# One fused decoder layer on one core: the shared step table is replaced by a table of its own for each engine

## The chip, the core and the metric

The kernel runs on one NeuronCore of a Trainium2 chip. The metric is the device time of one execution in microseconds; smaller is better. All data are fp32. Five engines take part: TensorE (PE, with its weight loads as PEld), VectorE (DVE), ScalarE (ACT), GpSimd (POOL) and SyncE (SP), which issues most DMAs.

## The reference, cut to what matters

```
x: (16, 128, 256)   ctx_1024: (16, 128, 256)          # 16 sequences of 128 tokens, 256 channels
x = x + attn(layernorm(x))        # latent attention: keys = values = x@latent_w (72 wide), 16 heads, causal softmax
x = x + birwkv(r=layernorm(x), k=ctx, v=ctx, w, u)    # two scans along time, sigmoid(r) * wkv
x = x + moe(layernorm(x))         # 8 experts, top 2 by sparsemixer, F=512, silu(gate)*up, down
```

## The kernel before, in words

The batch of 16 sequences is worked in 4 groups g of 4 sequences. Attention is cut into 64 **units** (sequence, quarter of the heads). One unit n runs through five engines: `S.n` scores on PE (mask and 8 matmuls), row maximum on DVE (L1197), four exponentials on ACT (`exps`, L983); `N.n` reciprocal of the sums on DVE (L1201) and the product with the exponentials on POOL (L1593); `T.n` transposes on PE (L739) and copy to `PT` on ACT (L988); `Y.n` mix with the values on PE (L748), copy to `ZT` on DVE (L1212) and, on SP, four DMAs that pack it into `zP` (L574). `O.b.i` is a quarter of the output projection of sequence b. `q.k.i` are five parts of the queries of a pair of sequences k: matmuls into one PSUM bank (L668), a biased copy on ACT (L976), a DMA by head into `qT` on SP (L561). As there is one bank, each part waits for the copy of the one before. `kt.g` and `va.g`/`vb.g` make keys and values.

The rest is threaded between the units. `bn`, `agg`, `rs`, `nmb`, `xn`, `tx` are a layernorm: statistics and shift on DVE, the power on POOL (`rs`, L1588), normalisation on ACT (L950), transposes on PE, copies. `w1` to `w8`, `wa`, `wb` are the bidirectional recurrence of a group and a half of the channels: exponential and scaling on ACT, four scans on DVE (`w2` to `w5`, L1236 and L1238), four sums on POOL (`w6`, `w7`), reciprocals on DVE (`w8`), product on POOL (`wa`), transposes and copy `wb`. `nr`, `sig`, `x2` apply the gate (`sig` is L1026 on ACT). `lg`, `r1` to `r3`, `ra`, `rw` route the tokens; `r4.g...` writes a group's two lists to HBM by eight indirect DMAs from POOL (L1636). After three groups `p1`, `p2`, `p3` plan the expert tiles; POOL then issues `gtk` (token lists, L1668), `gw` (weights of the first tile, L1660) and `lxg` (gathers, L1650). The expert stage with 23 tiles follows (`tg`, `up`, `si`, `hd`, `sh`, `dn`, `ao`, and `sw`, which splits weights: L1048 on ACT, L1132 on DVE), from about 392 us of the span.

The order is written out by hand in one table `STEPS` (L70 to L182), which `schedule()` turns into `ORDER` with a rule for the last tiles. Each of the five engine programs walks `ORDER` from first to last and issues its own part of each step, so all five have the same relative order. An engine is in order: a step that waits for a semaphore holds all its later steps. The count that a semaphore must reach is taken from a step's place in `ORDER` (`nth`).

In `ORDER` the beginning is: statistics, `tx.1.0`, constants, `kt.0`, then `q.0.0` to `q.0.4`, `va.0`, `S.0`, `S.1`, the normalisation of group 1, `S.2`, `T.0`, `q.1.0`, and so on. On POOL the end of the attention stage is: `N.55`, `rs.3.2`, `N.56`, `N.57`, `N.58`, the last two lists of group 1 (`r4.1.0.4.1.2`), `N.59`, `N.60`, six scatters of group 2, `N.61`, its last two, `rs.2.3.0.2`, `N.62`, `N.63`, `gtk.0`, `gtk.1`, `gw.0.0`. On ACT it is `T.60`, `sig.3.0.0`, `T.61`, `T.62`, `sw.0.0`, `T.63`.

## Time and profile before

| what | value |
|---|---|
| median of 3 runs | 604.07 us (602.4 to 605.44) |
| profiled execution | 600.46 us, of it span 598.8 us |
| granted TensorE clock, mean | 0.942 |
| instructions | 10336 |
| HBM read, written | 49.28 MB, 9.49 MB |

The profiled execution is 3.6 us below the median of the three runs. Busy shares stand for each engine; a busy PE is not PE at its peak, since ends of matmuls are modelled, and the weight loads (PEld) are the better measure of how densely the PE queue was fed.

### The profile page before, as it was taken

The numbers are of one execution on the slowest core, as the hardware profiler recorded it, in microseconds if no ns is written. First come the engines' busy times: TensorE is split into PE (matmuls) and PEld (weight loads), VectorE is DVE, ScalarE is ACT, GpSimd is POOL, SyncE is SP. The second block draws the span as 40 slices with busy tenths as digits, with TensorE's granted clock in tenths as the row PEclk, the third lists the DMA queues.
The fourth block names the chain that finished last, engine by engine and source line by source line (L and its number), as shares of the span: only waits on it lengthen the run. The fifth ranks groups of instructions, "written<-read, shape, count | busy, mean of one in ns | idle before, by whom it ended". The sixth has DMA issues, their size and how long they took to land.

```text
span 598.8 us, 10336 instructions
## 1 busy us (share of the span) xinstructions
PE 520.2 (87%) x3448; PEld 453.2 (76%) x3448; DVE 362.9 (61%) x740; ACT 329.9 (55%) x945; POOL 314.7 (53%) x277
## 2 busy tenths in 40 slices
...
GB/s 206 188 43 86 69 93 82 76 72 70 55 119 97 52 67 72 89 82 78 61 42 101 101 176 228 89 124 68 309 167 251 202 241 235 246 236 362 180 19 0
DMA packets 53219, 76.82 MB, mean 128 GB/s; under 512 B 10173, under 2 KB 41662, under 8 KB 52838
## 3 DMA queue, kind: packets, MB, share of 16 engines
...
q8 instruction: 27, 0.44, 0.3%
...
q10 hardware_dynamic: 804, 0.15, 0.1%
HBM read 49.28 MB, written 9.49 MB: 98 GB/s over the span
## 4 chain that ended last, share of the span: by engine, by line
PE 58%; DVE 9%; issue 9%; POOL 9%; DMA 7%; ACT 5%; SPq 2%; POOLq 0%; DVEq 0%; ACTq 0%
PE P L668 18%; PE PO L776 7%; PE P L731 6%; PE P L748 6%; PE PO L668 5%; PE P L739 3%; PE P L852 3%; POOL EB L1593 2%; DMA cxa<-xd,TK 2%; POOL cxa L1650 2%; ACT EB L983 2%; PE PO L861 2%; PE P L727 2%; PE P L686 1%; PE P L792 1%
## 5 line engine op out<-in xcount | busy, mean ns | idle before, releaser
L983 ACT ACTIVATE EB<-P,small 128x128 f32<-128x128 f32 x256 | 90.4, 369 | 74.7 <-DVE small L1197 64.6
L1593 POOL TENSOR_TENSOR EB<-EB,small 128x512 f32<-128x512 f32 x64 | 78.8, 1241 | 86.1 <-DVE small L1201 86.0
L668 PE MATMUL P<-GT,WF 128*128 128x256 f32 x768 | 101.9, 291 | 6.0 <-DVE GT L1132 2.6
L668 PEld LDWEIGHTS P<-GT,WF 128*128 128x128 f32 x768 | 97.4, 198 | 7.2 <-DVE GT L1132 3.1
L1677 POOL DMA_INDIRECT out<-Y,TK x39 | 65.8, 1687 | 65.2 <-DMA out<-Y,TK 29.2
L731 PEld LDWEIGHTS P<-KT,qT 72*128 72x128 f32 x512 | 69.8, 198 | 11.5 <-DMA qT<-qP 6.4
L748 PE MATMUL P<-PT,V 128*72 128x512 f32 x128 | 67.0, 605 | 9.7 <-ACT PT L988 8.2
L731 PE MATMUL P<-KT,qT 72*128 72x128 f32 x512 | 70.3, 282 | 5.1 <-DMA qT<-qP 5.1
L776 PE MATMUL PO<-Ow,zP 128*128 128x256 f32 x270 | 67.5, 390 | 2.7 <-DMA zP<-ZT 2.7
L1212 DVE COPY ZT<-P 72x512 f32<-72x512 f32 x64 | 43.3, 676 | 40.4 <-PE P L748 39.4
L776 PEld LDWEIGHTS PO<-Ow,zP 128*128 128x128 f32 x270 | 50.5, 195 | 15.9 <-issue 10.3
L1197 DVE TENSOR_REDUCE small<-P 128x4 f32<-128x512 f32 x64 | 43.3, 677 | 26.3 <-PE P L731 26.1
L1650 POOL DMA_INDIRECT cxa<-xd,TK x39 | 42.9, 1100 | 30.1 <-DMA TK<-xs 20.0
L668 PE MATMUL PO<-WF,HR 128*128 128x256 f32 x384 | 51.9, 294 | 4.5 <-issue 4.5
L988 ACT ACTIVATE PT<-P 128x512 f32<-128x512 f32 x64 | 38.8, 607 | 27.8 <-PE P L739 27.8
L668 PEld LDWEIGHTS PO<-WF,HR 128*128 128x128 f32 x384 | 49.9, 202 | 4.9 <-issue 4.9
L983 ACT ACTIVATION_READ_ACCUMULATOR EB<-P,small 128x1 f32 x256 | 52.9, 207 | 0.0
L1636 POOL DMA_INDIRECT xs<-TKS,SL x32 | 33.7, 1052 | 35.9 <-DVE TKS L1332 25.6
L739 PEld LDWEIGHTS P<-ident,EB 128*128 128x128 f32 x256 | 31.4, 144 | 22.1 <-issue 10.7
L739 PE MATMUL P<-ident,EB 128*128 128x128 f32 x256 | 39.9, 279 | 4.6 <-POOL EB L1593 4.5
L1077 ACT ACTIVATE Y<-PO,TK 128x256 f32<-128x256 f32 x39 | 16.7, 470 | 38.9 <-DMA out<-Y,TK 15.0
L976 ACT ACTIVATE qP<-P,small 128x256 f32<-128x256 f32 x72 | 30.9, 483 | 12.4 <-PE P L668 12.3
...
## 6 DMA issues: line engine op xcount, KB each, us to landing
WR<-wf SPq DMA_DIRECT2D x27, 512.0 KB, 4.9
arena<-wf SPq DMA_DIRECT2D x24, 512.0 KB, 4.9
...
WS<-wf SPq DMA_DIRECT2D x12, 512.0 KB, 7.8
...
X<-x SPq DMA_DIRECT2D x4, 512.0 KB, 5.9
cxa<-ctxin SPq DMA_DIRECT2D x4, 512.0 KB, 5.2
```

What stands on the lines that cost most here:

```text
L668: r = e.matmul(o, lt(a), rt_(b), start=start and n == 0, stop=stop and n == 2, skip_group_check=skip)
L731: p = e.matmul(S[:, 128 * j:128 * j + 128], qT[k % 2][:, 4 * hq + j, c:c + 128], KT[g % 2][:, r:r + 128], start=False, stop=True, skip_gro ...
L739: p = e.transpose(PTB[:, 128 * j:128 * j + 128], EB[n % 3][:, j, :], ident[:, :])
L748: e.matmul(YB[0:L, :], V[g % 2][:, b % GB, :], PT[n % 2][:, :], start=True, stop=True).then_inc(s_Y, 1)
L776: p = e.matmul(o, zP[b // NB % 2][:, m, 128 * (b % NB):128 * (b % NB) + 128], Ow[:, m, :], start=m == 0, stop=m == NQ - 1)
L983: e.activation(EB[i][:, j, :], S[:, 128 * j:128 * j + 128], ACT.Exp, bias=NM[i][:, j:j + 1], accum_out=SM[i][:, j:j + 1]).then_inc(s_exp, 1)
L988: e.activation(PT[n % 2][:, :], PTB[:, :], ACT.Copy).then_inc(s_pt, 1)
L1197: e.tensor_reduce(NM[n % 3], SB[n % 2][:, :].rearrange("p (h s) -> p h s", h=4), AX.X, ALU.max, negate=True).then_inc(s_max, 1)
L1212: e.tensor_copy(ZT[buf][:, :, c:c + 128], YB[0:L, :].rearrange("p (h t) -> p h t", h=4)).then_inc(s_z, 1)
L1593: e.tensor_tensor(EB[i][:, :, :], EB[i][:, :, :], SM[i].unsqueeze(2).broadcast_to([128, 4, 128]), ALU.mult).then_inc(s_prob, 1)
L1650: e.indirect_dma_start(XG[i][:, a_, :], None, xd[0:(TN * 3 // 4, TN + 1)[phase(j)], :], bass.IndirectOffsetOnAxis(ap=TK[:, j, a_, 0:1].bit ...
L1677: e.indirect_dma_start(outr, bass.IndirectOffsetOnAxis(ap=TK[:, j, a_, 0:1].bitcast(i32), axis=0), Y[j % 2][:, a_, :], None, bounds_check= ...
```

## The change

Five tables are added, `SYNC_STEPS`, `TENSOR_STEPS`, `VECTOR_STEPS`, `SCALAR_STEPS` and `GPSIMD_STEPS`, and a function `steps_of` that parses one. Each engine program walks its own table. `ORDER` and the semaphore counts stay. The steps are the same on every engine (181, 427, 511 of 518, 416 and 185 of them); the seven that are missing on DVE (`tg.16` to `tg.22`) issue nothing there. Against the old order 31, 145, 183, 109 and 47 of them are in another place. From `T.57` on PE, `S.62` on ACT, `Y.60` on DVE, `lxg.1` on POOL and `lw.3.1` on SP the tables are as before. One wait changes, in `add_x1`.

```diff
+SYNC_STEPS = """
+    ctx.0 q.0.0 q.0.1 q.0.2 q.0.3 q.0.4 q.1.0 q.1.1 ctx.1 q.1.2 q.1.3 q.1.4 Y.1 Y.3 Y.5 q.2.0 q.2.1 Y.7 q.2.2 q.2.3 q.2.4 Y.9 Y.11 q.3.0 ctx.2 Y.13
...
+    Y.51 Y.52 Y.53 Y.54 Y.55 out.0.0.4 out.1.0.4 out.2.0.4 xd.2.0.4 Y.56 owh Y.57 Y.58 Y.59 ltk.3 lw.2.0 lw.1.0 lw.1.1 lw.1.2 ltk.4 out.3.0.2 xd.3.0.2
+TENSOR_STEPS = """
+    tx.1.0.0.4.0 tx.1.0.0.4.1 q.0.0 q.0.1 kt.0 q.0.2 q.0.3 q.0.4 q.1.0 va.0 tx.1.1.0.4.0 S.0 S.1 S.2 S.3 S.4 T.0 q.1.1 T.1 Y.0 q.1.2 T.2 Y.1 q.1.3
+    tx.1.1.0.4.1 Y.2 S.5 T.3 q.1.4 S.6 Y.3 S.7 T.4 T.5 q.2.0 kt.1 Y.4 T.6 q.2.1 S.8 S.9 wb.0.0 Y.5 S.10 q.2.2 T.7 Y.6 T.8 S.11 S.12 q.2.3 Y.7 T.9 va.1
...
+VECTOR_STEPS = """
+    bn.1.0.0.0 bn.1.0.0.2 agg.1.0.0.4 nmb.1.0.0.4 split tx.1.0.0.4.0 tx.1.0.0.4.1 consts bn.1.1.0.0 bn.1.1.0.2 agg.1.1.0.4 nmb.1.1.0.4 w1.0.0 w2.0.0
+    w3.0.0 w4.0.0 w5.0.0 vb.0 S.0 S.1 N.0 tx.1.1.0.4.0 N.1 S.2 w1.0.1 N.2 S.3 S.4 w2.0.1 w3.0.1 w4.0.1 Y.0 w5.0.1 w8.0.0.0 w8.0.0.1 Y.1 N.3 w8.0.0.2
+    w8.0.0.3 Y.2 S.5 tx.1.1.0.4.1 N.4 N.5 S.6 N.6 S.7 bn.1.2.0.0 bn.1.2.0.2 Y.3 agg.1.2.0.4 bn.1.3.0.0 bn.1.3.0.2 N.7 Y.4 S.8 S.9 Y.5 w1.1.0 S.10 N.8
...
+SCALAR_STEPS = """
+    xn.1.0.0.0 xn.1.0.0.2 tx.1.0.0.4.0 consts tx.1.0.0.4.1 q.0.0 q.0.1 w1.0.0 w2.0.0 q.0.2 q.0.3 w4.0.0 q.0.4 kt.0 xn.1.1.0.0 xn.1.1.0.2 q.1.0
+    tx.1.1.0.4.0 w1.0.1 S.0 S.1 S.2 S.3 T.0 q.1.1 T.1 q.1.2 T.2 q.1.3 tx.1.1.0.4.1 S.4 T.3 S.5 S.6 q.1.4 T.4 w2.0.1 w4.0.1 T.5 q.2.0 kt.1 S.7 w1.1.0
...
+GPSIMD_STEPS = """
...
+    w7.2.1 N.27 N.28 N.29 x2.0.0.2.0 rs.3.0.0.4 N.30 N.31 N.32 N.33 wa.2.1 N.34 w6.3.0 N.35 N.36
+    N.37 N.38 N.39 w7.3.0 xb.6 N.40 N.41 wa.3.0 xb.7 N.42 N.43 rs.2.1.0.4 x2.1.0.0.0 x2.1.0.2.0 N.44 N.45 N.46 w6.3.1 rs.3.1.0.4 N.47 r4.0.0.4.0.0
+    r4.0.0.4.0.2 N.48 N.49 N.50 N.51 r4.0.0.4.1.0 rs.2.2.0.4 N.52 N.53 x2.2.0.0.0 x2.2.0.2.0 N.54 rs.3.2.0.4 N.55 r4.0.0.4.1.2 N.56 N.57 w7.3.1 wa.3.1
+    N.58 r4.1.0.4.0.0 N.59 N.60 r4.1.0.4.0.2 r4.1.0.4.1.0 r4.1.0.4.1.2 r4.2.0.4.0.0 r4.2.0.4.0.2 N.61 r4.2.0.4.1.0 r4.2.0.4.1.2 rs.2.3.0.2 N.62 N.63
+    gtk.0 gtk.1 gw.0.0 gw.0.1 gw.0.2 gtk.2 lxg.0 rs.3.3.0.2 lxg.1 rs.2.3.2.2 lxg.2 lxg.3 rs.3.3.2.2 r4.3.0.4.0.0 r4.3.0.4.0.2 lxg.4 r4.3.0.4.1.0
...
+def steps_of(table):
+
+    return [(name, *map(int, a)) for name, *a in (w.split(".") for w in table.split())]
...
-    order = [(name, *map(int, a)) for name, *a in (w.split(".") for w in STEPS.split())]
+    order = steps_of(STEPS)
...
-            for name, *a in ORDER:
+            for name, *a in steps_of(SYNC_STEPS):
...
-                ve_.wait_ge(s_xb, i + 1)
+                ve_.wait_ge(s_xb, nth("xb", i))
```

The other four engine loops change in the same way as the one of SyncE.

## Rows read from the trace of the kernel before

**Rows 1.** The page's first part: busy time, share of the span, instructions.

```profile
PE 520.2 (87%) x3448; PEld 453.2 (76%) x3448; DVE 362.9 (61%) x740; ACT 329.9 (55%) x945; POOL 314.7 (53%) x277
```

**Rows 2.** Windows: stretch, us, then busy of PE, PEld, DVE, ACT, POOL, clock, DMA.

```profile
32.00:72.00 40.00, 32.81 (x192) 27.35 (x190) 28.41 (x46) 25.51 (x93) 21.71 (x15) 0.83 0.22 67
72.00:150.00 78.00, 71.57 (x449) 56.10 (x449) 56.46 (x101) 52.89 (x195) 48.69 (x39) 1.00 0.25 76
150.00:270.00 120.00, 118.88 (x754) 98.94 (x753) 89.45 (x185) 79.08 (x283) 73.50 (x63) 1.00 0.26 80
270.00:318.00 48.00, 45.97 (x296) 37.70 (x295) 27.87 (x86) 30.31 (x118) 20.96 (x21) 1.00 0.24 69
318.00:362.00 44.00, 35.15 (x158) 25.15 (x157) 25.43 (x83) 13.76 (x47) 24.77 (x27) 0.88 0.46 123
```

**Rows 3.** Waits of the weight loads from 32 to 318 us: total, times, longest.

```profile
PEld P L739 <- POOL EB L1593: 9.5, 9, 1.9
PEld P L731 <- DMA qT<-qP: 6.4, 3, 3.4
PEld P L748 <- ACT PT L988: 5.4, 5, 2.2
```

**Rows 4.** Timeline of PE, the first units: start, duration, work, idle before.

```profile
17.38 2.83 PE L668 MATMUL P<-xnTa,Lw 128*72 128x512 f32 x6 [1.41 <-DVE xnTa L1132]
20.01 2.10 PE L668 MATMUL P<-xnTa,Wd 128*128 128x256 f32 x12
...
28.29 1.70 PE L668 MATMUL P<-xnTa,Wd 128*128 128x256 f32 x12 [0.93 <-ACT qP L976]
30.91 0.98 PE L668 MATMUL P<-xnTa,Wd 128*128 128x256 f32 x6 [0.93 <-ACT qP L976]
...
35.57 2.07 PE L731 MATMUL P<-KT,qT 72*128 72x128 f32 x8 [3.14 <-DMA qT<-qP]
...
72.62 0.48 PE L727 MATMUL P<-maskr,identr 128*128 128x512 f32 x1
```

**Rows 5.** Timeline of ACT, the first units.

```profile
31.94 0.47 ACT L976 ACTIVATE qP<-P,small 128x256 f32<-128x256 f32 x1 [1.07 <-PE P L668]
...
38.40 0.37 ACT L983 ACTIVATE EB<-P,small 128x128 f32<-128x128 f32 x1 [5.48 <-DVE small L1197]
...
42.53 2.08 ACT L950 ACTIVATE XN<-X,small 128x256 f32<-128x256 f32 x4
...
50.32 0.37 ACT L983 ACTIVATE EB<-P,small 128x128 f32<-128x128 f32 x1 [0.94 <-DVE small L1197]
...
63.26 0.37 ACT L983 ACTIVATE EB<-P,small 128x128 f32<-128x128 f32 x1 [1.99 <-DVE small L1197]
```

**Rows 6.** Timeline of POOL, one row of unit 5 and the last units.

```profile
60.48 3.00 POOL L1593 TENSOR_TENSOR EB<-EB,small 128x512 f32<-128x512 f32 x1 [7.36 <-DVE small L1201]
...
323.77 1.53 POOL L1593 TENSOR_TENSOR EB<-EB,small 128x512 f32<-128x512 f32 x1 [1.26 <-DVE small L1201]
...
332.02 0.96 POOL L1636 DMA_INDIRECT xs<-TKS,SL  x1 [0.30 <-issue]
333.00 1.05 POOL L1593 TENSOR_TENSOR EB<-EB,small 128x512 f32<-128x512 f32 x1
...
338.04 0.72 POOL L1588 TENSOR_TENSOR small<-small 128x2 f32<-128x2 f32 x1 [1.55 <-DVE small L1173]
...
341.23 0.65 POOL L1668 DMA_DIRECT2D TK<-xs  x1 [0.45 <-issue]
...
343.65 0.54 POOL L1660 DMA_DIRECT2D arena<-wf  x1 [0.67 <-issue]
```

**Rows 7.** Timeline of ACT in the same stretch.

```profile
340.83 1.09 ACT L1026 ACTIVATE EX<-X,small 128x256 f32<-128x256 f32 x2 [3.32 <-DVE small L1249]
344.54 0.60 ACT L988 ACTIVATE PT<-P 128x512 f32<-128x512 f32 x1 [2.61 <-PE P L739]
```

**Rows 8.** The page's sixth part: KB of each DMA, median us to landing.

```profile
arena<-wf POOLq DMA_DIRECT2D x3, 512.0 KB, 6.2
```

More of the change, by code:

```diff
@@ L182 @@
 """
+SYNC_STEPS = """
+    ctx.0 q.0.0 q.0.1 q.0.2 q.0.3 q.0.4 q.1.0 q.1.1 ctx.1 q.1.2 q.1.3 q.1.4 Y.1 Y.3 Y.5 q.2.0 q.2.1 Y.7 q.2.2 q.2.3 q.2.4 Y.9 Y.11 q.3.0 ctx.2 Y.13
+    Y.15 q.3.1 q.3.2 Y.17 q.3.3 q.3.4 Y.19 ctx.3 Y.21 Y.23 q.4.0 q.4.1 q.4.2 q.4.3 q.4.4 Y.25 q.5.0 Y.27 xd.0.0.4 Y.29 Y.31 q.5.1 q.5.2 q.5.3 q.5.4
+    Y.33 Y.35 Y.37 q.6.0 Y.39 Y.40 q.6.1 q.6.2 q.6.3 q.6.4 Y.41 Y.42 Y.43 Y.44 Y.45 Y.46 q.7.0 q.7.1 q.7.2 Y.47 xd.1.0.4 Y.48 Y.49 q.7.3 q.7.4 Y.50
+    Y.51 Y.52 Y.53 Y.54 Y.55 out.0.0.4 out.1.0.4 out.2.0.4 xd.2.0.4 Y.56 owh Y.57 Y.58 Y.59 ltk.3 lw.2.0 lw.1.0 lw.1.1 lw.1.2 ltk.4 out.3.0.2 xd.3.0.2
+    lw.2.1 out.3.2.2 lw.2.2 lw.3.0 xd.3.2.2 lw.3.1 lw.3.2 lw.4.0 lw.4.1 ltk.5 lw.5.0 lw.5.1 ltk.6 ltk.7 lw.4.2 lw.6.0 lw.6.1 lw.5.2 lw.7.0 lw.7.1
+    lw.6.2 ltk.8 ltk.9 ltk.10 lw.8.0 lw.8.1 lw.7.2 lw.9.0 lw.9.1 lw.8.2 lw.10.0 lw.10.1 lw.9.2 lw.11.0 lw.11.1 ltk.11 lw.10.2 ltk.12 lw.12.0 lw.12.1
+    lw.11.2 ltk.13 lw.13.0 lw.13.1 lw.12.2 ltk.14 lw.14.0 lw.14.1 lw.13.2 ltk.15 lw.15.0 lw.15.1 lw.14.2 ltk.16 lw.17.0 lw.17.1 lw.15.2 lw.16.0
+    lw.16.1 lw.16.2 ltk.17 lw.18.0 lw.18.1 lw.17.2 ltk.18 lw.18.2 lw.19.0 lw.19.1 lw.19.2 lw.20.0 lw.20.1 lw.20.2 ltk.19 lw.21.0 lw.21.1 lw.21.2
+    lw.22.0 lw.22.1 lw.22.2 ltk.20 ltk.21 ltk.22
@@ new lines @@
+"""
+GPSIMD_STEPS = """
+    rs.1.0.0.4 q.0.0 rs.1.1.0.4 w6.0.0 w7.0.0 N.0 N.1 xb.2 xb.3 N.2 xb.0 N.3 N.4 N.5 wa.0.0 N.6 N.7 w6.0.1 w7.0.1 N.8 rs.1.2.0.4 N.9 N.10 wa.0.1
+    w6.1.0 w7.1.0 N.11 N.12 wa.1.0 w6.1.1 N.13 N.14 N.15 N.16 w7.1.1 N.17 N.18 N.19 N.20 wa.1.1 w6.2.0 w7.2.0 N.21 N.22 xb.1 N.23 rs.1.3.0.4 N.24 N.25
+    xb.4 wa.2.0 xb.5 rs.2.0.0.4 x2.0.0.0.0 N.26 w6.2.1 w7.2.1 N.27 N.28 N.29 x2.0.0.2.0 rs.3.0.0.4 N.30 N.31 N.32 N.33 wa.2.1 N.34 w6.3.0 N.35 N.36
+    N.37 N.38 N.39 w7.3.0 xb.6 N.40 N.41 wa.3.0 xb.7 N.42 N.43 rs.2.1.0.4 x2.1.0.0.0 x2.1.0.2.0 N.44 N.45 N.46 w6.3.1 rs.3.1.0.4 N.47 r4.0.0.4.0.0
+    r4.0.0.4.0.2 N.48 N.49 N.50 N.51 r4.0.0.4.1.0 rs.2.2.0.4 N.52 N.53 x2.2.0.0.0 x2.2.0.2.0 N.54 rs.3.2.0.4 N.55 r4.0.0.4.1.2 N.56 N.57 w7.3.1 wa.3.1
+    N.58 r4.1.0.4.0.0 N.59 N.60 r4.1.0.4.0.2 r4.1.0.4.1.0 r4.1.0.4.1.2 r4.2.0.4.0.0 r4.2.0.4.0.2 N.61 r4.2.0.4.1.0 r4.2.0.4.1.2 rs.2.3.0.2 N.62 N.63
+    gtk.0 gtk.1 gw.0.0 gw.0.1 gw.0.2 gtk.2 lxg.0 rs.3.3.0.2 lxg.1 rs.2.3.2.2 lxg.2 lxg.3 rs.3.3.2.2 r4.3.0.4.0.0 r4.3.0.4.0.2 lxg.4 r4.3.0.4.1.0
+    r4.3.0.4.1.2 ao.0 ao.1 lxg.5 lxg.6 lxg.7 ao.2 lxg.8 ao.3 lxg.9 lxg.10 ao.4 ao.5 ao.6 lxg.11 ao.7 lxg.12 ao.8 lxg.13 ao.9 lxg.14 ao.10 lxg.15 ao.11
+    lxg.16 ao.12 lxg.17 ao.13 lxg.18 ao.14 lxg.19 ao.15 lxg.20 ao.16 lxg.21 ao.17 lxg.22 ao.18 ao.19 ao.20 ao.21 ao.22
@@ L185, in schedule @@
+"""
+def steps_of(table):
+    return [(name, *map(int, a)) for name, *a in (w.split(".") for w in table.split())]
 def schedule():
-    order = [(name, *map(int, a)) for name, *a in (w.split(".") for w in STEPS.split())]
+    order = steps_of(STEPS)
     def emit(*step):
@@ L875, in down @@
                 p.then_inc(s_dn, 1)
-            for name, *a in ORDER:
+            for name, *a in steps_of(TENSOR_STEPS):
                 if name == "tx":
@@ L1077, in weigh @@
                     e.activation(Y[j % 2][:, a_, :], PO[:, j % 2, C * a_:C * a_ + C], ACT.Copy, scale=TK[:, j, a_, 1:2]).then_inc(s_y, 1)
-            for name, *a in ORDER:
+            for name, *a in steps_of(SCALAR_STEPS):
                 if name == "consts":
@@ L1468, in hidden_lo @@
                 sub_lo(r[:, 1], HF[n][:, :].rearrange("p (f t) -> p f t", f=2), r[:, 0]).then_inc(s_hrlo, 1)
-            for s in ORDER:
+            for s in steps_of(VECTOR_STEPS):
                 name, a = s[0], s[1:]
```

60 lines of the change are left out of this document (added).

## The prediction, made before the result was known

> **What bounds the kernel now.** I read the page's busy shares first. No engine but PE is near full: PE 87%, its weight loads 76%, DVE 61%, ACT 55%, POOL 53% [rows 1]. A busy PE is not a dense PE, so the second view is the windows of the attention stage, by weight loads. They fill 56.10 of 78 us (72%) between 72 and 150 us, but 98.94 of 120 (82%) between 150 and 270 us and 37.70 of 48 (79%) from there to 318 us [rows 2]. DVE, ACT and POOL stand at 58 to 75% in these windows. So in the attention stage the time is set by no one's throughput. It is set by how the five in-order queues interlock: unit after unit goes PE, DVE, ACT, DVE, POOL, PE, ACT, PE, DVE, and whatever stands in front of a ready step in its queue delays it. The third view, the waits of the weight loads, shows the joints: 9.5 us for POOL's product of a unit, 6.4 us for the queries' DMA, 5.4 us for ACT's copy of the transposed probabilities [rows 3]. These 21 us are the part of the holes that has a name. That makes an order an edit with a price, and it bounds it: if all of 72 to 150 were as dense as 150 to 270, 56.10 / 0.8245 = 68.0 us would do for 78, a gain of 10.0 us; the stretch to 318 us would give 2.3 us. What follows from 392 us on is the experts; its steps are in the same order and only start earlier or later.
>
> **The change part by part.**
>
> **1. The first queries (all engines, up to unit 9).** Before, the keys run first (17.38), the first query part starts at 20.01, and since the next part waits for ACT's copy, each takes a turn of 2.63 us (28.29 to 30.91); the last copy ends at 32.41, and the head-wise DMA lands for the scores at 35.57 [rows 4, 5]. After, two query parts come before the keys: 17.38 and 20.01, the keys in the gap behind them until about 24.1 (six matmuls at the 0.44 us in which they went before: 2.63 us from 17.38 to 20.01), then three parts at 24.1, 26.7 and 29.4. The last starts 1.5 us earlier than 30.91. On ACT the early `w1`, `w2` and `w4` stand between the copies. They need the context and the cleared decay table, and each fits into the idle time of a query turn, so I cost them at nothing; if the table came late, each us would be a us of the queries. Then `q.1.0`, the normalisation of group 1 (2.08 us on ACT, at 42.53 before, [rows 5]) and a transpose are done while the DMA flies (3.14 us of idle PE before, [rows 4]) and the first four scans of DVE run in time that was empty. The exponentials of unit 0 then start near 37.0 for 38.40. Walking on with the durations of the old trace, in the new order: ACT runs units 0 to 2 back to back until 42.5, stands until `T.0`, which is now behind `S.4`, is done (45.2), runs unit 3 at 45.2 for 50.32 before, the three query turns, unit 4 near 54.7, unit 5 at 57.1 for 63.26 before [rows 5], unit 7 until 66.9, and `S.9` starts at 67.2 for 72.62 [rows 4]. That is 5.4 us earlier. The clock is in this too: it was 0.83 of full in the mean from 32 to 72 us [rows 2]. If it falls as before, the sum stands; if it doesn't fall, some 3 us more are gained, and if it stays low twice as long, 3 us are lost. I take 5.4 us, with 2 and 8 as ends.
>
> **2. The middle (units 10 to 56).** Here the order is new nearly everywhere on PE and DVE, in small steps: on PE the scores stand ahead of the transposes and mixes of older units, the projection is drawn into whole runs, and query parts come earlier; on DVE the reciprocals `w8`, the scans and the statistics are moved to where a unit's row maximum or copy does not need the engine; the copies `wb` of groups 1 to 3, whose readers are far behind, move up to 40 steps later on ACT. Nothing is added or removed, so only holes can go. On the upper side stand the 10.0 us of 72 to 150 and the 2.3 us of 270 to 318. On the lower side nothing excludes a loss: a unit's steps are held by longer runs at some places. For example, four statistics steps are now ahead of `N.7` on DVE, and three scans ahead of `Y.0`. As the stretch from 150 to 270 already is at 82% I expect nothing of it. From 72 to 150 I take half of the way, 5.0 us, because the named waits (21 us over the whole stage, [rows 3]) are half of what the holes add up to; the ends are a loss of 4 and a gain of 12.
>
> **3. SP's stores.** `out.0` and `out.1` go from between the packs of units 27 and 42 to behind `Y.55`, with `out.2`. Their readers are the first additions of expert results, far later. Between `Y.55` and `Y.56` SP's queue has time; I cost it at nothing. If the packing DMAs of units 56 to 59 were held by the stores, `O.14` would be late by what is left of three transfers, at most some 3 us.
>
> **4. POOL's lists.** This part costs. Six scatters of group 1 are moved from before `N.58` to behind `N.60`, ahead of all of group 2. One costs 1.26 us (0.96 and 0.30 of issue, [rows 6]). Before, from the end of `N.60` (325.30) to `gtk.0` (341.23) POOL had eight scatters, three unit products and one `rs`: 8 x 1.26 + 3 x 1.05 + 0.72 = 13.9 us in 15.9 us [rows 6]. After it has fourteen scatters: 21.5 us, and `gtk.0` starts 5.6 us later measured from `N.60`. `N.61`, `N.62` and `N.63` have the room for that, for PE takes them up late (the copy of `T.61` is at 344.54, [rows 7]; the product was done at 334.05, [rows 6]). `rs.2.3.0.2` has not: it goes from 338.04 to about 344.0, the gate `sig.3.0.0` follows it by 2.8 us (340.83), so it ends near 347.9, and the copy of `T.61` stands behind it on ACT: 347.9 for 344.54, or 346.6 if the two small DVE steps between run undisturbed. That is 2.1 to 3.4 us on the chain to the experts. The weights of the first tile are requested at 349.3 for 343.65 and land 6.2 us later (355.5, [rows 6, 8]), just when ACT would take them up. I take +3.0 us, between 0 (if POOL comes to `N.60` earlier against the others) and +6.0. `w7.3.1` and `wa.3.1`, three sums before `N.58`, go into POOL's idle time there.
>
> **5. The changed wait of `add_x1`, the parse function, the missing `tg` on DVE:** no time.
>
> **Sum.** -5.4 - 5.0 + 3.0 = -7.4 us. Against the profiled execution, 600.46 us, of which 598.8 are span, this is 593.1 us; it lay 3.6 us below the median of its runs, so against the median of 604.07 us I forecast **596.7 us**.
>
> **The rivals.** (a) **The middle is dense enough in any order**: the first part gives 5.4 us, the lists take 3.0, and the rest stays: 601.7 us. For it speaks that 150 to 270 has no slack to speak of, against it the 72% of the stretch before. (b) **The whole gain comes**: 10.0 + 2.3 in the middle, 5.4 at the head, no loss at the lists as POOL is early: 17.7 us, 586.4 us. (c) **Slower: the lists of POOL.** In 318 to 362 us the span of the attention stage is already held together by small steps (weight loads 25.15 of 44 us, [rows 2]). If POOL has no idle time left before `N.60`, since `w7.3.1`, `wa.3.1` and the scatters of group 0 were moved there too, all six scatters come through, 6 x 1.26 = 7.6 us, and from the point where the head and the middle together give less than that, the kernel is slower. With 2.0 at the head and 0 in the middle: 609.7 us. With it goes the meeting of scans and products: the product of unit 5 took 3.00 us where others take 1.05, beside two scans [rows 6], 1.95 us for one meeting; four more such meetings on the path would cost 7.8 us. The Trainium skill, page "SBUF — State Buffer", section "Who interferes with whom", says that a DVE instruction with two SBUF inputs contends with a GpSimd instruction that reads SBUF, and that the one that issues first holds the port for its whole instruction. By that rule bunching the scans, as three in a row before `Y.0`, speaks against this change; by the rule the trace agrees, since that product ended only when two scans in a row had. (d) **It does not do what it says**: DMA landings and waits shift the real arrival of steps against what the tables assume, and gains and losses cancel; 603 us.
>
> **How the numbers follow.** Forecast 0.45 (591 to 600); (a) and (d) together 0.27; (b) 0.13; (c) 0.15. The range that leaves out 2 in 10 reaches from 587.0, just above (b), to 607.0, halfway into (c). About 0.5% (3.0 us) is what a measurement of this kernel can tell from no change. Faster by more than that means below 601.05: the forecast, (b), and a part of (a): 0.62. Within it: 0.24. Slower: 0.14.
>
> **What would show it right or wrong.** In the profile after, the first row maximum's exponentials on ACT should start near 37 us and `S.9` near 67 us. The weight loads from 72 to 150 us should fill 76 to 78% of their window. `S.56`, `S.63` and the first `L1660` on POOL should be 10, 10 and 5 us earlier than before; if the distance from the product of `N.60` to the first `L1668` is not near 21.5 us, step 4 is wrong. The gate at 340.83 should follow an `rs` that had to wait for scatters rather than for DVE. The experts' stretch should have the same length. The prediction fails if the half-clock stretch at the start grows, if PE's waits for POOL's products grow beyond 9.5 us, or if the packing DMAs of units 56 to 59 are late.

## The result

After the change the kernel takes 612.83 us (median of four runs, 610.47 to 613.21); the kernel before, run beside it, 604.44. The ratio is 1.0155, with an interval of 1.0105 to 1.0205: **slower, by 8 to 9 us**, where the forecast was 596.7 and the range ended at 607. The profiled execution took 613.21 us, span 611.5. All ratios in this document leave out, as a slower state, the executions that took over 1.5% more than the fastest of the same kernel; two profiles below are of such executions, with the mask matmuls twice (610.84 us) and with the cut at unit 33 (609.46 us). The same kernel ran once more beside some of the experiments:

> The kernel after once more, beside the others on this chip: for the ratio on the same footing and for the stretch from 336 to 343 us, where the first profile has the results of TensorE's last scores 6 us late. If that lateness belongs to this order it is there again; if it was an event of that one execution, it is gone and N.61 still begins at about 342, since GpSimd's block of indirect DMAs holds it by itself. Time 1.0155 of the kernel before either way.

Measured 1.0143 (1.0089 to 1.0196). The late results of the last scores, told of at the end, were gone and `N.61` began at 342.84 all the same (342.29 in the first profile), so the loss does not need that event.

The busy shares of the page say almost nothing. PE stood at 87% before [rows 1], and after the change the row reads:

```profile
PE 522.4 (85%) x3448; PEld 452.2 (74%) x3448; DVE 360.2 (59%) x740; ACT 329.9 (54%) x945; POOL 319.8 (52%) x277
```

The windows of the kernel after, same stretches and columns as [rows 2] (length, then busy of PE, PEld, DVE, ACT, POOL, the clock, DMA), say more:

```profile
32.00:72.00 40.00, 34.37 (x239) 28.40 (x237) 28.02 (x53) 27.95 (x110) 20.90 (x18) 1.00 0.20 63
72.00:150.00 78.00, 71.11 (x430) 56.26 (x429) 58.50 (x91) 49.99 (x182) 48.62 (x35) 0.98 0.24 75
150.00:270.00 120.00, 114.38 (x715) 92.51 (x714) 76.70 (x173) 73.95 (x265) 63.19 (x53) 1.00 0.22 66
270.00:318.00 48.00, 44.55 (x260) 35.03 (x259) 27.94 (x84) 29.03 (x110) 20.10 (x19) 0.96 0.24 68
318.00:362.00 44.00, 32.31 (x161) 23.93 (x160) 24.64 (x84) 14.76 (x59) 31.89 (x36) 0.81 0.48 133
```

Read the first two columns, stretch less PE busy. Before, TensorE was idle 7.2 us of 32 to 72, 6.4 of 72 to 150, 1.1 of 150 to 270 and 2.0 of 270 to 318 [rows 2]. After, it is idle 5.6, 6.9, 5.6 and 3.5 us. The head has won 1.6 us of idle time and also the clock (1.00 for 0.83 [rows 2]); from 150 us on the idle time has grown by 5.9 us, from 3.1 to 9.1.

For the middle as a whole I cut both traces at the same two steps, the end of the mix of unit 11 and the end of the mix of unit 55. First the kernel before, then the kernel after:

```profile
103.30:312.10 208.80, 202.44 (x1268) 165.65 (x1269) 147.71 (x314) 136.86 (x495) 116.34 (x101) 1.00 0.25 73
```

```profile
97.60:315.60 218.00, 205.21 (x1248) 164.62 (x1247) 139.98 (x310) 134.96 (x494) 110.62 (x93) 0.98 0.23 69
```

Unit 11 ends 5.7 us earlier, unit 55 ends 3.5 us later: **the middle is 9.2 us longer**, 6.4 of it idle time of TensorE (12.8 for 6.4 us) and 2.8 its busy time. The busy time can be the clock: the mean of 0.98 comes from two stretches of 3.4 us each, from 142.9 and from 282.8 us, in which the granted clock was 1.2 GHz in place of 2.4. Each can cost up to 1.7 us; the window before has none.

Cut once more at the end of the mix of unit 41, first before, then after:

```profile
103.30:245.00 141.70, 137.37 (x874) 112.68 (x875) 106.69 (x206) 95.04 (x345) 83.09 (x70) 1.00 0.25 75
245.00:312.10 67.10, 65.06 (x397) 52.97 (x396) 41.02 (x108) 41.82 (x152) 33.25 (x31) 1.00 0.24 70
```

```profile
97.60:243.35 145.75, 138.83 (x859) 112.00 (x858) 96.29 (x187) 92.54 (x341) 75.54 (x61) 0.99 0.22 70
243.35:315.60 72.25, 66.38 (x390) 52.62 (x389) 43.69 (x124) 42.42 (x155) 35.08 (x32) 0.98 0.23 67
```

At the end of the mix of unit 41 both kernels have run about the same number of matmuls from the start (1310 and 1311), and the kernel after is still 1.7 us ahead. Up to there it has lost 4.0 us of its lead, 2.6 of them in idle time; behind it, it loses 5.2 us, 3.8 of them in idle time. Between the mixes of units 41 and 48 TensorE was idle 4.4 us (40.85 less 36.47), where before it was busy all 39.6. The new idle time is thus not spread evenly.

The tail follows. From unit 55's mix to unit 63's it was 44.7 us and is 50.1. The expert stage's first matmul comes at 373.40 for 364.48, and the last 3.8 us of the difference between the two profiled executions (12.7) arise among the experts. The second profile of the same kernel, 607.48 us, has the same 373.40 for the first expert matmul and does not have these 3.8 us.

### The profile page after: what moved, and what is told of

The parts are those of the page before. It is cut to its first block, busy times and chain, and to the rows that moved or that the text cites. A ratio compares the mean times of both kernels' runs of the same rounds, so it can differ in the third digit from the quotient of the medians.

```text
span 611.5 us, 10348 instructions
## 1 busy us (share of the span) xinstructions
PE 522.4 (85%) x3448; PEld 452.2 (74%) x3448; DVE 360.2 (59%) x740; ACT 329.9 (54%) x945; POOL 319.8 (52%) x277
## 4 chain that ended last, share of the span: by engine, by line
PE 36%; DMA 15%; DVE 14%; issue 14%; POOL 12%; ACT 5%; another core or an unknown queue 1%; POOLq 1%; SPq 0%; DVEq 0%; ACTq 0%
DMA out<-Y,TK 12%; PE P L770 10%; PE PO L878 6%; PE P L850 5%; PE P L833 4%; POOL EB L1695 3%; PE P L841 3%; PE PO L770 2%; DVE ZT L1314 2%; POOL cxa L1752 2%; POOL out L1779 1%; POOL X L1729 1%; ACT XN L1052 1%; DVE small L1299 1%; PE P L829 1%
## 5 line engine op out<-in xcount | busy, mean ns | idle before, releaser
L1695 POOL TENSOR_TENSOR EB<-EB,small 128x512 f32<-128x512 f32 x64 | 71.5, 1127 | 109.6 <-DVE small L1303 109.5
L850 PE MATMUL P<-PT,V 128*72 128x512 f32 x128 | 68.6, 618 | 15.6 <-issue 9.0
L833 PEld LDWEIGHTS P<-KT,qT 72*128 72x128 f32 x512 | 67.3, 191 | 7.1 <-issue 4.3
L833 PE MATMUL P<-KT,qT 72*128 72x128 f32 x512 | 67.5, 274 | 0.0
L1752 POOL DMA_INDIRECT cxa<-xd,TK x39 | 44.4, 1138 | 26.4 <-DMA TK<-xs 16.3
L1085 ACT ACTIVATION_READ_ACCUMULATOR EB<-P,small 128x1 f32 x256 | 54.7, 214 | 0.0
L841 PEld LDWEIGHTS P<-ident,EB 128*128 128x128 f32 x256 | 30.1, 144 | 26.5 <-issue 15.3
L1738 POOL DMA_INDIRECT xs<-TKS,SL x32 | 32.2, 1006 | 25.5 <-DVE TKS L1434 17.0
```

What stands on the lines that cost most here:

```text
L833: p = e.matmul(S[:, 128 * j:128 * j + 128], qT[k % 2][:, 4 * hq + j, c:c + 128], KT[g % 2][:, r:r + 128], start=False, stop=True, skip_gro ...
L841: p = e.transpose(PTB[:, 128 * j:128 * j + 128], EB[n % 3][:, j, :], ident[:, :])
L850: e.matmul(YB[0:L, :], V[g % 2][:, b % GB, :], PT[n % 2][:, :], start=True, stop=True).then_inc(s_Y, 1)
L1085: e.activation(EB[i][:, j, :], S[:, 128 * j:128 * j + 128], ACT.Exp, bias=NM[i][:, j:j + 1], accum_out=SM[i][:, j:j + 1]).then_inc(s_exp, 1)
L1695: e.tensor_tensor(EB[i][:, :, :], EB[i][:, :, :], SM[i].unsqueeze(2).broadcast_to([128, 4, 128]), ALU.mult).then_inc(s_prob, 1)
L1752: e.indirect_dma_start(XG[i][:, a_, :], None, xd[0:(TN * 3 // 4, TN + 1)[phase(j)], :], bass.IndirectOffsetOnAxis(ap=TK[:, j, a_, 0:1].bit ...
```

## The experiments

All kernels whose tables are mixed from the two share the code of the kernel after; only the tables differ. Each had five rounds beside the kernel before, which took 601 us in them; ratios are to it. "Cut at unit n" means that every table is new up to that unit's step and in the old order from there.

### The head alone

```
tables of after up to T:Y.11 V:Y.11 A:T.12 G:N.13 S:Y.11, then the order of before
```

> Every table in the new order up to unit 11 (TensorE and VectorE up to their step Y.11, ScalarE to T.12, GpSimd to N.13, the SP queue to Y.11), from there the order of the kernel before. Measured so far: 604.4 before, 612.8 after. Theory A (the end follows TensorE's own idle time, not its weight loads' share): in the two profiles TensorE stood idle 30.8 us of the first 110 before and 27.9 us after, so this kernel gains those 2.9 us and keeps them, about 601.5. Theory B (the forecast's first term, weight loads at 76 to 78% are headroom and the head alone is worth 5.4 us): 599. Theory C (what the head wins is given back as soon as it meets the dense stretch, whatever the order there): 604.4.

Measured 0.9964 (0.9929 to 0.9998). The profile shows why it is less than expected: the cut has a seam. PE's timeline there:

```profile
102.85 1.05 PE L852 MATMUL P<-PT,V 128*72 128x512 f32 x2 [1.48 <-DVE ZT L1316]
106.02 0.66 PE L843 MATMUL P<-ident,EB 128*128 128x128 f32 x4 [2.12 <-POOL EB L1697]
```

`Y.12` follows `Y.11` with only a transpose between and waits 1.48 us for VectorE's copy; `T.13` waits 2.12 us for its row product. I mended it in two later runs with these steps:

```
-Y.11 T.12 Y.12 T.13 S.16 Y.13 T.14 S.17 q.3.1 Y.14 O.1.0 O.1.1
+Y.11 T.12 S.16 q.3.1 Y.12 O.1.0 T.13 O.1.1 Y.13 T.14 S.17 Y.14
```

> The kernel of the last run without its tail edit: the new order up to unit 11 with the seam mended, then the order before; sig.3.0.0 and O.14.0 stand ahead of T.61 again. Measured: 0.9884 with both, 0.995 with the tail edit alone. Theory A (head and tail add, and the head's 3.4 us that the last profile shows from unit 17 on reach the end): 0.9934 (0.991 to 0.996), 597 us. Theory C (the head is only worth something once the tail is mended, since the stretch from 333 to 350 us waits for the lists in any case): 0.998 to 1.000.

Measured 0.9929 (0.9893 to 0.9965), 4.3 us (2.1 to 6.4) faster than the kernel before. In its profile the scores, exponentials, products and mixes of units 20 to 55 are 2.5 to 2.8 us earlier than before. The head's gain is real and is carried through two hundred microseconds of old order.

### The middle alone, and half of it

```
before up to unit 11, after's order from there to unit 55, before's again
```

> The order before up to unit 11, the new order from there to unit 55 on every engine, then the order before again. Theory A (TensorE has next to no idle time from 110 to 318 us before, 5.1 us, and the new order makes it 12.2 by placing transposes and mixes where their inputs are late): +7.1, about 611.5. Theory B (the forecast's second term, -5.0): 599.4. Theory C (the two orders are equal in the middle and the loss lies in the tail alone): 604.4.

Measured 1.0319 (1.0266 to 1.0371), 19 us, far beyond both theories. Its two seams share in that: unit 55 is 11.4 us late in its profile, unit 56 already 25, since `wb.3.1` then waits 5.5 us for GpSimd's `wa.3.1` and the row products behind it. The part without seams is the stretch from unit 11 to 55, 220.4 us for 208.8, with 13.5 us of idle time of TensorE for 6.4, much as in the kernel after.

> Every table in the new order up to unit 33, then the order before. With the same cut at unit 11 the ratio was 0.9964. Theory A (in the middle each stretch of the new order adds idle time of TensorE; of the 9 us lost from unit 11 to 55 in the two profiles some half, 5, lie before unit 33): ratio about 1.004 to 1.006, 604 to 605. Theory C2 (the whole loss is at the late seams and lists, behind unit 41): 0.996, as with the cut at 11.

Measured 1.004 (1.0001 to 1.0079), in size as theory A said. With the head at 0.993 this kernel has lost 6 to 7 us against the head alone, but its profile gives most of that to the seam. From the mix of unit 33 to that of unit 41 it took 41.10 us, where the kernel with the head alone took 38.70 (TensorE idle 4.3 us for 0.2), with a half-clock stretch of 3.4 us from 214.2 us. The run shows that an order cut at unit 33 is no faster than the old one. How much of the loss the new order makes by itself before unit 34 it does not show.

### Is TensorE dense in the middle?

```
+                masked = not 16 <= n < 48
+                if masked:
                     e.matmul(S[:, :], identr[:, :], maskr[...], start=True, stop=False, ...)
```

> The kernel before without the mask matmul of units 16 to 47 (32 matmuls of 128 x 512; their scores are left unmasked, so the output is another). Theory A (TensorE is dense from 110 to 318 us, its 0.23 us of stream for each mask matmul is on the path): 32 x 0.234 = 7.5 us less than the kernel before, ratio about 0.988. Theory B (the forecast's reading: the weight loads' share of 76 to 83% leaves slack, waits on other engines set the pace): at most 2 us less, ratio above 0.996, and TensorE's idle time there grows by the rest.

Measured 0.9914 (0.987 to 0.9957): 5.2 us less. And the other way round, the same matmul twice:

```
+                for _ in range(2 if 16 <= n < 48 else 1):
```

> The kernel before with the mask matmul of units 16 to 47 issued twice (32 more matmuls of 128 x 512, the same result). Theory A (TensorE is dense there): 32 x 0.234 us = 7.5 us more, less what its 1 to 3 us of idle time takes in, ratio 1.008 to 1.0125. Theory B (the forecast's reading, 17 to 24 per cent of slack behind the weight loads' share): at most 2 us, ratio under 1.004. Leaving the same 32 matmuls out gave 0.9914.

Measured 1.0049 (1.0004 to 1.0094): 2.9 us more (0.2 to 5.6). That is between the two theories and settles neither. Both intervals are wide, so I read the profiles from the mix of unit 15 to that of unit 47, in which all 32 matmuls lie. Before, with them twice, and without them:

```profile
122.60:276.40 153.80, 150.75 (x949) 123.60 (x948) 111.33 (x223) 101.31 (x359) 88.69 (x76) 1.00 0.26 80
```

```profile
127.40:287.50 160.10, 158.38 (x978) 130.08 (x977) 111.50 (x223) 101.81 (x359) 87.09 (x76) 0.99 0.25 77
```

```profile
121.20:276.10 154.90, 148.04 (x921) 120.80 (x921) 111.40 (x223) 102.06 (x360) 93.43 (x77) 0.98 0.26 80
```

Twice makes the stretch 6.3 us longer for 7.5 us of matmuls, while the idle time falls from 3.1 to 1.7 us. A half-clock stretch of 3.4 us lies in it, up to 1.7 us of the 6.3, and the profile is of the second longest of twelve executions (599.6 to 612.2 us), so 6.3 is an upper reading. Leaving them out opens idle time (6.9 for 3.1 us) and a half-clock stretch of 6.8 us fell into it, so the stretch isn't shorter at all (154.90 for 153.80). The 5.2 us of that kernel do not show in this stretch of its profile: its first expert matmul is 1.7 us earlier than before, and 3.9 us of its 5.6 us arise among the experts. What the three profiles do show is that little idle time is left: 7.5 us of extra matmuls found 1.3 us of it to fill. That added work costs between 2.9 us (the runs) and 6.3 us (the profile) of 7.5 speaks against the 18% of slack that the weight loads' share had promised from 150 to 270 us. That removed work would come back in full is not shown.

### Filling TensorE's waits

In the kernel after, the new idle time stands at places where two steps of one kind meet or a transpose is early. PE's timeline of its second profile:

```profile
103.27 0.66 PE L841 MATMUL P<-ident,EB 128*128 128x128 f32 x4 [0.83 <-POOL EB L1695]
112.38 1.08 PE L850 MATMUL P<-PT,V 128*72 128x512 f32 x2 [0.78 <-DVE ZT L1314]
...
144.07 1.12 PE L841 MATMUL P<-ident,EB 128*128 128x128 f32 x4 [1.27 <-POOL EB L1695]
...
185.98 1.05 PE L850 MATMUL P<-PT,V 128*72 128x512 f32 x2 [0.87 <-DVE ZT L1314]
...
253.78 0.66 PE L841 MATMUL P<-ident,EB 128*128 128x128 f32 x4 [1.22 <-POOL EB L1695]
262.86 0.63 PE L841 MATMUL P<-ident,EB 128*128 128x128 f32 x4 [1.31 <-ACT PT L1090]
```

`Y.14` right behind `Y.13` waits 0.78 us, because both use one bank and VectorE must copy the first out; `Y.30` and `Y.36` do the same. The edit, in part:

```
-O.1.0 T.13 O.1.1 ... Y.13 Y.14 S.19 Y.15 T.16 q.3.2 ... T.21 T.22 O.3.1 q.4.0 S.26 O.3.2
+O.1.0 O.1.1 T.13 ... Y.13 S.19 Y.14 q.3.2 Y.15 T.16 ... O.3.1 T.21 q.4.0 O.3.2 T.22 S.26
-S.34 Y.29 Y.30 ... Y.35 Y.36 q.6.0 ... T.44 S.47 O.9.2 ... T.48 T.49 Y.48 q.7.3 Y.49 O.10.2 T.50
+Y.29 S.34 Y.30 ... Y.35 q.6.0 Y.36 ... S.47 O.9.2 T.44 ... T.48 q.7.3 T.49 O.10.2 Y.48 O.10.3 Y.49 T.50
```

> The kernel after with seven places of TensorE's table between units 13 and 50 reordered so that work that is ready stands between two mixes or two transposes in a row (Y.13 Y.14, T.21 T.22, Y.29 Y.30, Y.35 Y.36, T.48 T.49 Y.48) or ahead of a transpose whose row product is late (T.13, T.44), and ScalarE's copy of T.44 ahead of its two normalisations xn.3.1. In the profile after these places hold 9.4 us of TensorE's idle time. Theory A (TensorE's idle time in the dense middle is what the new order costs): the idle time from 110 to 318 us falls from 12 to about 5 us and the kernel by 5 to 7 us, ratio to the kernel before 1.003 to 1.006 (after: 1.0143). Theory E (the waits are those of a loop in which another engine is late anyway; filling one moves it to the next place): ratio 1.012 to 1.015, idle time unchanged.

Measured 1.0125 (1.0094 to 1.0157): the kernel after, within the measurement. Theory E holds. The waits of PE from 100 to 318 us, first of the kernel after (second profile), then with the fillings:

```profile
PE P L841 <- POOL EB L1695: 5.6, 8, 1.3
PE P L850 <- DVE ZT L1314: 3.8, 5, 0.9
PE P L841 <- ACT PT L1090: 2.3, 3, 1.3
```

```profile
PE P L830 <- ACT EB L1086: 3.6, 3, 2.1
PE P L789 <- ACT XN L1053: 2.0, 2, 1.8
PE P L851 <- DVE ZT L1315: 1.8, 2, 1.5
...
PE P L842 <- POOL EB L1696: 1.1, 2, 0.9
```

The waits for products fell from 5.6 to 1.1 us, and new ones for exponentials (a score moved behind two fillers, before its bank was free) and for ACT's normalisation took their place; the idle time between units 11 and 55 went from 12.7 to 12.3 us. So the idle time is not made where it is seen; where it is made this run does not tell.

### The tail: GpSimd's lists

```
before's tables; only these on GpSimd (part):
-N.49 r4.1.0.4.0.0 N.50 N.51 r4.1.0.4.0.2 N.52 r4.1.0.4.1.0 ... N.58 r4.1.0.4.1.2 N.59 N.60 r4.2...
+N.58 r4.1.0.4.0.0 N.59 N.60 r4.1.0.4.0.2 r4.1.0.4.1.0 r4.1.0.4.1.2 r4.2.0.4.0.0 r4.2.0.4.0.2 N.61
```

> The kernel before with GpSimd's twelve list scatters of groups 0 to 2 alone moved, to where the new table has them (between the same row products; up to six in a row ahead of N.61). Everything else as before. Theory A (the scatters are cheap as long as N.61 to N.63 are not late by more than the block): 604.4 to 606. Theory D (the block of scatters ahead of N.61 brings the stall of 4.5 to 4.7 us that the profile after shows at 338 to 342.7 us): about 609. The forecast had +3.0 for this, 607.4.

Measured 1.010 (1.0059 to 1.0142), 6.0 us, nearer to theory D's 4.6 than to A's 1.6 at most. The block in the kernel after (second profile), POOL's timeline:

```profile
329.24 1.04 POOL L1695 TENSOR_TENSOR EB<-EB,small 128x512 f32<-128x512 f32 x1 [1.86 <-DVE small L1303]
330.43 1.00 POOL L1738 DMA_INDIRECT xs<-TKS,SL  x1 [0.15 <-issue]
...
341.86 0.96 POOL L1738 DMA_INDIRECT xs<-TKS,SL  x1 [0.30 <-issue]
342.84 1.05 POOL L1695 TENSOR_TENSOR EB<-EB,small 128x512 f32<-128x512 f32 x1
...
348.88 0.73 POOL L1690 TENSOR_TENSOR small<-small 128x2 f32<-128x2 f32 x1
...
351.97 0.66 POOL L1770 DMA_DIRECT2D TK<-xs  x1 [0.35 <-issue]
```

Ten scatters stand between `N.60` and `N.61` (the expectation said six), four more behind it, and `rs.2.3.0.2` comes at 348.88 for 338.04 [rows 6]. ACT in the same profile:

```profile
351.75 1.09 ACT L1128 ACTIVATE EX<-X,small 128x256 f32<-128x256 f32 x2 [10.66 <-DVE small L1351]
352.75 0.57 ACT L1090 ACTIVATE PT<-P 128x512 f32<-128x512 f32 x1
```

The gate `sig.3.0.0` (L1128) waits 10.66 us and the copy of `T.61` goes right behind it, as the forecast had it: 352.75 for 344.54 [rows 7].

Two edits of the kernel after at this place. In the first, two scatter steps went ahead of `w7.3.1`, which holds `wb.3.1` on TensorE:

```
-N.57 w7.3.1 wa.3.1 N.58 r4.1.0.4.0.0 N.59 N.60 r4.1.0.4.0.2 r4.1.0.4.1.0 r4.1.0.4.1.2 r4.2...
+N.57 r4.1.0.4.0.0 r4.1.0.4.0.2 w7.3.1 wa.3.1 N.58 r4.1.0.4.1.0 N.59 r4.1.0.4.1.2 N.60 r4.2...
```

> The kernel after with the six scatters between N.57 and N.61 spread: two ahead of N.58 and one each behind N.58 and N.59, so that two stand between N.60 and N.61 in place of five. Everything else as after, 612.8. Theory D (the block brings the stall): the 4.7 us go, about 608.1. Theory A (the stall in TensorE's own results at 336 to 342.7 us has another cause): 612.8 within 1, with the stall still there or gone by itself.

Measured 1.0183 (1.0133 to 1.0233), no gain: TensorE now waits 5.0 us at `wb.3.1` for GpSimd's sum. The edit moved the price instead of removing it. The second has the sums out of the way first:

```
GpSimd:  N.50 w7.3.1 N.51 ... r4.0.0.4.1.0 wa.3.1 rs.2.2.0.4 ... N.57 r4.1.0.4.0.0 r4.1.0.4.0.2
         N.58 r4.1.0.4.1.0 r4.1.0.4.1.2 N.59 N.60 r4.2.0.4.0.0 r4.2.0.4.0.2 r4.2.0.4.1.0 r4.2.0.4.1.2 N.61
VectorE: w8.3.1.2 w8.3.1.3 (was behind Y.53)
```

> The kernel after with GpSimd's tail undone: the context products of k 1 of group 3 (w7.3.1, wa.3.1) go from behind N.57 to behind N.50 and behind the first scatter pair of N.51, VectorE's w8.3.1.3 goes from behind Y.53 to behind w8.3.1.2, four scatters go ahead of N.58 and N.59 and the other four stand between N.60 and N.61, so that N.61 has 4 instead of 5 pairs' worth of work in a row before it. Theory D (the block of ten indirect DMAs, 329.9 to 342.3 us in the profile after, holds N.61 by 4.9 us and with it the last transposes): N.61 comes about 5 us earlier and the kernel takes 608. Theory A2 (the end hangs on something else there, the block is hidden): 612.8 within 1.

Measured 1.0127 (1.009 to 1.0164). `rs.2.3.0.2` moved from 348.88 to 343.27, and unit 63's mix is 7.1 us behind the kernel before in place of 8.9. But `O.14.0` then waits 4.77 us for the packing DMA of `Z` in front of `T.61`. I count this as a small gain that the runs do not separate from none.

### T.61 ahead of the two waits

```
before's tables; TensorE:  -Y.60 O.14.0 T.61 Y.61 O.14.1   +Y.60 T.61 Y.61 O.14.0 O.14.1
                 ScalarE:  -T.60 sig.3.0.0 T.61            +T.60 T.61 sig.3.0.0
```

> The kernel before with two steps moved in its tail: TensorE takes T.61 and Y.61 ahead of O.14.0 (which waits for the packing DMA of Z), ScalarE copies T.61 ahead of sig.3.0.0 (which waits for GpSimd's rs.2.3.0.2 behind the list scatters). Theory F (these two waits, 2.1 and 3.3 us in the profile before, are where late lists reach the path, and T.61 sits behind both although its row product is ready 9 us earlier): T.61 is copied 4 us earlier and the kernel is 2 to 4 us faster, ratio 0.993 to 0.997. Rival G (T.61 to T.63 are not on the path there, the expert rows and weights are): 1.000.

Measured 0.995 (0.9912 to 0.9989), as theory F says. The transpose starts at 340.29 for 343.44, the copy follows at 341.39 for 344.54 [rows 7]. Of these 3.1 us only 1.1 reach the first expert matmul (363.40 for 364.48):

```profile
341.39 0.60 ACT L1092 ACTIVATE PT<-P 128x512 f32<-128x512 f32 x1 [2.92 <-PE P L843]
341.88 1.08 ACT L1130 ACTIVATE EX<-X,small 128x256 f32<-128x256 f32 x2
```

Is this also the only way by which late lists reach the end? Then the same edit should hide them. Both edits together, the move of the lists and this one:

> The kernel before with the twelve list scatters moved as in the run of the lists alone (that cost 1.0 per cent) and T.61 ahead of O.14.0 and sig.3.0.0 (that gave 0.5 per cent without the move). Theory F (the late scatters reach the path through rs.2.3.0.2, sig.3.0.0 and ScalarE's copy of T.61 behind it; with the copy ahead of it they are hidden): 0.995 to 1.000, nearly all of the 1.0 per cent gone. Theory D (they reach it through the row products N.61 to N.63, which are still behind the block): 1.005.

Measured 1.0138 (1.0088 to 1.0188): theory F fails here. In ACT's timeline the next late thing has taken the lead:

```profile
341.68 0.60 ACT L1092 ACTIVATE PT<-P 128x512 f32<-128x512 f32 x1 [4.00 <-PE P L843]
...
355.48 1.06 ACT L1152 ACTIVATE WF<-arena 128x1024 fp32r<-128x1024 f32 x1 [4.36 <-DMA arena<-wf]
356.44 0.58 ACT L1092 ACTIVATE PT<-P 128x512 f32<-128x512 f32 x1
```

`T.61` is copied 2.9 us earlier than in the kernel before, but `sw.0.0` (L1152) waits for the first expert's weights, which GpSimd requests behind the scatters (351.61 for 343.65 [rows 6]), and the copy of `T.63` stands behind it. From 356.4 to 372 us TensorE was busy 11.15 of 15.6 us, and its granted clock was the lower one (1.2 GHz) from 356.4 us for 41 us.

```
-T.62 sw.0.0 T.63
+T.62 T.63 sw.0.0        (ScalarE, on top of the last kernel)
```

> The kernel before with the late list scatters and T.61 ahead of O.14.0 and sig.3.0.0, as in the run that gave 1.0138, and now ScalarE's copy of T.63 ahead of sw.0.0 too. In that run's profile the copy of T.61 came 2.9 us before that of the kernel before, but T.63's copy stood 3.0 us behind it, right after sw.0.0, which waits for the first expert's weights, whose loads GpSimd issues after the scatters and the first row loads (8 us late). Theory I (one late thing after another takes the lead, sw.0.0 next): T.63 is copied at about 352, Y.63 ends about 3 us earlier, and the first expert matmul, 371.6 us there, comes 0 to 3 us earlier: ratio 1.006 to 1.0135. Theory J (the gathered rows, behind the same scatters, set the expert stage's start by themselves): T.63 early, the first expert matmul still at 371 and the ratio as it was.

Measured 1.0145 (1.0106 to 1.0184). No answer: in this profile TensorE's results of the last scores are 7.6 us late (below), so `T.63` was copied at 359.6 and not at 352. That the first expert matmul nevertheless came at 371.9, where it was at 371.6, speaks for theory J, but the clock differed between the two. Which of the two chains sets the start of the experts stays open; that both hang on the same scatters is shown.

### The SP queue

The kernel after with `SYNC_STEPS` in the order of the kernel before:

> The kernel after with the SP queue's table of the kernel before, that is with the stores of groups 0 and 1 (512 KB each) back at units 27 and 42 instead of behind Y.55, and the query and packing transfers where they were. After measured 1.0143. Forecast's term for the queue: 0, up to 3 us if the two stores meet the packing transfers and the first expert loads around 320 to 340 us. Theory H (they do: the share of the DMA engines from 318 to 337 us is 0.57 after, 0.45 before, and O.14.0 waits for a packing transfer there): 1.009 to 1.011. Theory A: 1.0143 within 0.003.

Measured 1.0672 (1.0619 to 1.0725), outside both theories: 40 us slower than the kernel before, some 32 us slower than the kernel after. Waits of PE from 32 to 318 us:

```profile
PE P L833 <- DMA qT<-qP: 17.1, 3, 6.9
PE P L841 <- ACT PT L1090: 5.1, 7, 1.1
PE P L850 <- DVE ZT L1314: 4.8, 7, 1.0
PE PO L878 <- DMA zP<-ZT: 4.0, 1, 4.0
```

The scores of a new head group wait three times for the queries' transfer, up to 6.9 us, as it is queued behind a transfer that waits for VectorE. Twice, the longest wait among them, that is a load of the context (L647), at which the queue stood 8.6 and 11.4 us; once it is a packing transfer, at which it stood 5.7 us. The small moves on that queue, which I had not priced, are needed by the rest of the change.

```
-Y.54 Y.55 out.0.0.4 out.1.0.4 out.2.0.4     +q.4.4 out.0.0.4 Y.25 ... Y.41 out.1.0.4 Y.42 ... Y.55 out.2.0.4
```

> The kernel after with the two 512 KB stores alone back at their old places on the SP queue (out.0.0.4 behind q.4.4, out.1.0.4 behind Y.41), everything else of its table new. After: 1.0143. Putting the whole old table of that queue back cost 5 per cent more, so the swaps of its small steps belong to the order of the others; this run asks for the stores alone. Theory A (the forecast's 0: the stores are off the path at both places): 1.0143 within 0.003. Theory H (behind Y.55 they hold the packing transfers that O.14.0 and O.15 wait for): 1.008 to 1.011.

Measured 1.0239 (1.019 to 1.0288). The stores at their new place cost nothing that these runs show; the two intervals overlap by a hair, and this profile too has the late results described at the end, 9.4 us of them, so I don't call the new place a gain.

### All mended, and the best version

The kernel after with the fillings, `T.61` first, the sums earlier and the scatters spread (two steps of group 2 ahead of `N.61`, two behind):

> The kernel after with all of it: the filled places of TensorE's middle, the list scatters spread with w7.3.1 and wa.3.1 earlier, and T.61 ahead of O.14.0 and sig.3.0.0. Theory A with F: 1.0143 less about 6 us for the middle and 5 for the tail: ratio 0.996 to 1.000. If middle and tail hang on something that none of these edits touch: 1.010 or more.

Measured 1.0039 (1.0007 to 1.0072): 6 us better than the kernel after. Its middle is as before, 216.9 us with 12.1 us idle; all of the gain is in the tail, where unit 63's mix is 4.2 us late in place of 8.9.

The cut at unit 11 with its seam mended, and `T.61` first:

> The new order up to unit 11, then the order before with one place mended at the seam (the first cut had 1.5 and 2.1 us of TensorE's idle time at Y.12 and T.13, where two steps followed each other with nothing between), and T.61 ahead of O.14.0 and sig.3.0.0. Theory A with F: the head's 2.9 us are kept now and the tail gives 2 to 4: ratio 0.989 to 0.993, faster than both kernels. Theory C (the head's gain cannot be kept, and the tail is off the path): 0.996.

Measured **0.9884** (0.9843 to 0.9924), 594.4 us for 601.1: faster than both kernels. It has the new order for eleven units, the old one for the rest, and `T.61` ahead of `O.14.0` and `sig.3.0.0`. The middle, same two steps as above:

```profile
99.90:310.30 210.40, 203.29 (x1252) 164.77 (x1251) 142.41 (x309) 136.28 (x495) 117.72 (x102) 0.98 0.25 76
```

## Why the prediction was wrong

**1. The head (forecast -5.4, ends -2 and -8): right, somewhat large.** The exponentials of unit 0 start at 35.62 (forecast 37.0, before 38.40), `S.9` at 67.17 (67.2). Alone the head is worth 4.3 us. That `S.9` came out so exactly is luck. The 5.4 us stood for a clock that falls as before, and some 3 us more were to come if it did not fall; it did not (1.00 for 0.83 [rows 2]), so by the forecast's own working some 8 us were due. And this profile is the earliest of the twelve that have the new head: in them `S.9` starts at 67.17 to 70.94, in the mean at 69.4, and in the eight with the old head at 72.06 to 73.55, in the mean at 72.7, which is 3.3 us. The clock was at its lower level for 13.7 us before 60 us in all eight old ones; of the twelve new ones eight have no such time, two have 3.4 us, and two have 10.2 and 13.7 us. Besides, `S.9` overstates the gain, since the new order puts scores first; what counts is how much of TensorE's work is done.

**2. The middle (forecast -5.0, ends +4 and -12): the failed step; measured +9.2.** The mistake is in the first paragraph of the forecast: "A busy PE is not a dense PE", so I took the weight loads' share, 72 and 82% [rows 2], and called the rest holes. The column beside it had the answer: 71.57 of 78 and 118.88 of 120. From 72 to 150 us TensorE was idle 6.4 us before, and from 110 to 318 us 5.1 us, so by this reading the 10.0 us by which I bounded the gain did not exist. Adding 7.5 us of matmuls to units 16 to 47 cost 2.9 us (the runs) to 6.3 us (the stretch in the profile). The reason for taking half was wrong too: the named waits, 21 us, are a third of the holes that the weight loads' rows add up to from 32 to 318 us (65.9 us [rows 2]), not half. On the other side, I bounded the loss at 4 us without a reason, and it was 9.2: 6.4 us of new idle time and up to 3.4 us from two half-clock stretches. 4.4 of the 6.4 us lie between the mixes of units 41 and 48. I could not pin it to single steps: filling the seven visible waits left it unchanged (12.3 for 12.7 us). That the old order had each step arrive when its input did, so that 145 moved steps on TensorE could mostly lose, is my reading and not shown. Which of the five tables makes the loss stays open: only SP's was put back alone, and that cost 5% more.

**3. SP's stores (forecast 0): nothing against it.** But I had priced only the two stores and not the 29 other moved steps on that queue; the old order of the whole queue among the new ones costs some 32 us.

**4. The lists (forecast +3.0, ends 0 and +6): mechanism right, size half.** From the end of `N.60` to the first row load it is 21.8 us (forecast 21.5). The gate, the copy of `T.61` and the weights are late in the order in which the working had them. Moving the lists alone cost 6.0 us (3.5 to 8.5). The term was sized at `T.61` only; the first weights' request (353.89 for 343.65 [rows 6]) and with it `sw.0.0` and `T.63` were said to arrive "just when ACT would take them up", and they hold the path when `T.61` does not. Besides, POOL came to `N.60` 4.4 us later than before, not earlier, as the middle had lost.

**The sum.** -4.3 for the head, +9.2 in the profile of the middle and +6.0 for the lists give +10.9, for +8.4 to +9.4 measured; as runs and a profile are mixed in it, it is a rough check and no proof that the parts add. **Rivals.** (a) had the middle unchanged and (c) named the right mechanism for a slower kernel with half of the loss in it (609.7 us); neither had the middle lose. The port meetings in (c) played no part that I can show: DVE's and POOL's own busy times in the middle are not longer (139.98 for 147.71, 110.62 for 116.34).

**The signs.** Most of the signs that I had named came out against the forecast. The weight loads fill 56.26 of 78 us from 72 to 150 us, 72% as before and not 76 to 78%. `S.56` starts 2.8 us later (303.43), `S.63` 4.2 us later (335.56) and the first weights' request 10.2 us later, where 10, 10 and 5 us earlier were forecast. The weight loads' waits for GpSimd's products grew to 10.4 us, beyond the 9.5 of [rows 3]. The half-clock stretch at the start did not grow, it went away. The distance from `N.60` to the first row load and the gate behind the late `rs` came as forecast. One reading in the working is also wrong: GpSimd was busy 44% from 270 to 318 us [rows 2], below the 58 to 75% given for the three engines.
